# x copied into the output, and each tile's rows added into it by one accumulating scatter

## The chip, the core and the metric

The kernel runs on one core of a Trainium2 chip. The metric is the device time of one execution in microseconds (us), as the median of several runs. A profile of one execution gives, for each engine, when each instruction ran and what it waited for. The engines are PE (TensorE, matmul; its weight loads are PEld), DVE (VectorE), ACT (ScalarE), POOL (GpSimd) and SP (SyncE, which here only issues DMAs).

## What is computed

x is 4 batches of 1024 tokens with 1024 features. From x, a softmax over its rows and two outer factors (`side`, `cond`) a score is made for each of the 1024 x 1024 places of a batch, the diagonal is left out, and the 10240 highest places get a 1: that is the mask. The mask's rows are then the inputs of a mixture of eight experts, of which each token takes two, and the result is added to x:

```python
def reference(x, side, cond, G, gate_w, up_w, down_w, lora_A, lora_B):
    adj = side * cond * softmax(x) / sqrt(1024)       # diagonal: -inf
    m = ones at the 10240 highest places of each batch, else 0
    w = the two highest of softmax(m @ G), at their experts, else 0
    gated = silu(m @ gate_w[e].T) * (m @ up_w[e].T)
    out = sum over e of w[e] * (gated @ down_w[e].T + (m @ lora_A[e].T) @ lora_B[e].T)
    return x + out
```

## The kernel before

**Batches and tiles.** The four batches run one after another. A batch's 2048 pairs of token and expert are sorted by expert into T = 23 tiles of 128 slots, each tile of one expert. Since each expert's last tile is seldom full, and since 23 tiles are enough for any split, some slots hold no pair and the last tiles can be empty. While the tiles of batch n run, DVE, ACT and POOL find the mask of batch n + 1 between them, at places that tables of numbers set (`DVE_COUNT_AT`, `BELOW_AT` and others); then `route(n + 1)` on DVE makes the tables of the next batch: for each slot of each tile the row of the mask to gather (`mask_row`) and the row to write to (`put_row`).

**One tile.** POOL issues an indirect DMA that gathers 128 rows of the mask from DRAM into `xg` (`gather`, L511, three buffers, asked for three tiles ahead). PE turns them (L665), ACT stores them as `xt` (L837), PE multiplies by the first layer (L678), ACT and DVE make the gated product, PE multiplies by the second (L701 to L704), and ACT stores the result, scaled, in `y` (`store_y`, L850, two halves a tile, two buffers, NY = 2). POOL then issues an indirect DMA that writes the 128 rows of `y` to DRAM (`put_out`, L519). A slot without a pair has a row number beyond the bound, and its row is not written.

**From the put rows to the output.** `put_rows` has a row for each of the 2 x 1024 pairs of token and role (first and second expert), in two copies by turns. While batch n + 1 runs, batch n's rows are put together in 16 pieces of 128 x 512: SP loads a piece of x and the two pieces of put rows that belong to it (`load_piece`, L364 and L366), POOL adds them up (`sum_piece`, L528 and L531), and SP stores the sum in the output (`store_piece`, L373). `PIECE_AT` says after which tile POOL takes which piece. The last batch has no batch behind it: its x is loaded once more into `v`, its put rows go to the place of the first layer's weights (`last_put`, L420), DVE adds them (L1445) and SP stores the sums (L423).

**What sets the order.** Each engine takes its instructions in the written order and waits on semaphores; DMAs from SP stand in one queue, those from POOL in another. ACT waits ahead of a y store until the put of two tiles before has landed (`put`). POOL never waits for a put. SP's `move_mask(n)` waits for the mask of batch n, then loads the x of the next batch (4 MB) and stores the mask (2 MB).

Of the kernel before, what the change touches and what calls it, by code (L numbers as in the profile page):

```python
# [14 lines left out]
P = 128  # L15
# [13 lines left out]
SKIP = 4096.0  # L29
# [4 lines left out]
def build(nc, x, side, cond, G, gate_w, up_w, down_w, lora_A, lora_B, out):  # L34
# [37 lines left out]
    PIECES, NC = 2 * C, 2  # L72
# [29 lines left out]
    PIECE_AT = {**{j + 1: j for j in range(9)}, **{j + 4: j for j in range(9, PIECES)}}  # L102
    PIECES_FIRST = 14

    with ExitStack() as ctx:
# [24 lines left out]
        piece = sb("piece", [P, NC, 3, HALF], F32)  # L130
# [18 lines left out]
        spare = piece[:, :, :, :].rearrange("p i k h -> p (i k h)")  # L149
# [52 lines left out]
        none_here, second_here = temp(T), temp(T)  # L202
# [10 lines left out]
        expert_no, tile_no, token_1 = cell(E), cell(T), cell(C)  # L213
        lower = cell(E * E).rearrange("p (a e) -> p a e", a=E)
# [20 lines left out]
        def table_of(n, i, dt=F32):  # L235
# [3 lines left out]
        put_row = [table_of(n, 1, I32) for n in range(B)]  # L239
        g_scale = [table_of(n, 2) for n in range(B)]  # L240
        y_scale = [table_of(n, 3) for n in range(B)]
        expert = [table_of(n, 4, I32) for n in range(B)]
# [26 lines left out]
        put_rows = [nc.dram_tensor(f"put_rows{i}", [ROLES * S, H], F32, kind="Internal").ap() for i in range(2)]  # L269

# [24 lines left out]
        put = [sem(f"put{i}") for i in range(NY)]  # L295
        piece_landed = [sem(f"piece_landed{i}") for i in range(NC)]
        piece_stored = [sem(f"piece_stored{i}") for i in range(NC)]
        half_summed, summed_piece = sem("half_summed"), sem("summed_piece")
        last_x_landed = [sem(f"last_x_landed{c}") for c in range(C)]
        rows_landed = [sem(f"rows_landed{c}") for c in range(C)]  # L300
        last_summed, last_stored = sem("last_summed"), sem("last_stored")
# [6 lines left out]
        out_rows = out.rearrange("b (p c) h -> b p c h", c=C)  # L308
        put_roles = [a.rearrange("(r p c) h -> r p c h", r=ROLES, c=C) for a in put_rows]

        last_put = [[w1_raw[:, c, r * 2 * H:(r + 1) * 2 * H].bitcast(F32) for r in range(ROLES)]
                    for c in range(C)]
# [12 lines left out]
        def _(sp):  # L325
# [27 lines left out]
            def wait_put(n):  # L353

                for i in range(NY):
                    sp.wait_ge(put[i], 16 * len(range(i, T * (n + 1), NY)))

            def load_piece(n, j):
                u = PIECES * n + j
                at, c, half = u % NC, j // 2, j % 2  # L360
                cols = slice(half * HALF, (half + 1) * HALF)
                if u >= NC:
                    sp.wait_ge(piece_stored[at], 16 * (u // NC))
                sp.dma_start(piece[:, at, 0, :], x_rows[n][:, c, cols]).then_inc(piece_landed[at], 16)  # L364
                for r in range(ROLES):
                    sp.dma_start(piece[:, at, 1 + r, :],  # L366
                                 put_roles[n % 2][r][:, c, cols]).then_inc(piece_landed[at], 16)

            def store_piece(n, j):
                u = PIECES * n + j  # L370
                c, half = j // 2, j % 2
                sp.wait_ge(summed_piece, u + 1)
                sp.dma_start(out_rows[n][:, c, half * HALF:(half + 1) * HALF],  # L373
                             piece[:, u % NC, 0, :]).then_inc(piece_stored[u % NC], 16)
# [19 lines left out]
            for n in range(B):  # L394

                more = n + 1 < B
                if n == 0:
                    move_mask(1)
                else:
                    if n == 1:  # L400

                        sp.wait_ge(b_turned, 4)
                        sp.wait_ge(a_turned, 1)
                    wait_put(n - 1)
                    for j in range(PIECES + NC):
                        if j >= NC:
                            store_piece(n - 1, j - NC)
                        if j < PIECES:
                            load_piece(n - 1, j)
                        if more and j == PIECES_FIRST + NC - 1:  # L410
                            move_mask(n + 1)
                if n + 2 < B:
                    sp.wait_ge(scores_ready, n + 2)
                    load_t(n + 2)

            n = B - 1
            wait_put(n)
            for c in range(C):
                for r in range(ROLES):
                    sp.dma_start(last_put[c][r], put_roles[n % 2][r][:, c, :]).then_inc(rows_landed[c], 16)  # L420
            for c in range(C):
                sp.wait_ge(last_summed, c + 1)
                sp.dma_start(out_rows[n][:, c, :], v[:, c, :]).then_inc(last_stored, 16)  # L423
            sp.wait_ge(last_stored, 16 * C)
            for i in range(NC):
                sp.wait_ge(piece_stored[i], 16 * len(range(i, PIECES * (B - 1), NC)))

        @block.gpsimd
        def _(pool):
# [9 lines left out]
            nc.gpsimd.iota(token_1.bitcast(I32), pattern=[[1, C]], base=1, channel_multiplier=C)  # L439
            nc.gpsimd.iota(slot_int.bitcast(I32), pattern=[[1, P]], base=0, channel_multiplier=0)  # L440
# [7 lines left out]
            for ints in (expert_no, tile_no, token_1):  # L448
                nc.gpsimd.tensor_copy(ints, ints.bitcast(I32))
            nc.gpsimd.tensor_copy(slot_no[:, :], slot_int.bitcast(I32))  # L450
            pool.drain()
# [72 lines left out]
            def sum_piece(n, j):  # L524
                u = PIECES * n + j
                at = u % NC
                pool.wait_ge(piece_landed[at], 48 * (u // NC + 1))
                nc.gpsimd.tensor_tensor(piece[:, at, 0, :], piece[:, at, 0, :], piece[:, at, 1, :],  # L528
# [947 lines left out]
```

## Time and profile before

| | |
|---|---|
| median of 3 runs | 812.58 us (808.84 to 816.08) |
| span of the profiled execution, first to last instruction | 807.6 us |
| PE, DVE, ACT, POOL busy | 521.7, 515.2, 453.9, 390.2 us |
| DMA by SP's queue | 108.60 MB, 39.0% of 16 engines' span |
| DMA by POOL's queue | 50.37 MB, 17.9% of 16 engines' span |
| granted clock of PE, mean | 0.844 |

The profiled execution's own time is shown as this span; the median of the runs, which hold the launch's own time beside it, is 5.0 us above. Times in the rows count from the span's start. An engine's busy time is a mean over stages with different limits, so the stages are read one by one. A DMA's landing is counted from the start of the instruction that issues it to the last update of its semaphore.

### The profile page before, as it was taken

The page shows a single profiled execution, that of the slowest core. Times are in us where ns is not written, and L with a number is a line of the kernel's source. Part 1 is how long each engine was busy: PE and PEld are TensorE (multiplying, and loading weights), DVE is VectorE, ACT ScalarE, POOL GpSimd, SP SyncE. Part 2 cuts the span into 40 slices and gives each one's busy share as a digit, 9 for nine tenths or more (in the row PEclk, how much of TensorE's full clock was granted, in tenths as well). Part 3 has the DMA queues.
Part 4 walks back from the last instruction along what each step waited for, and adds up shares of the span by engine and source line. Part 5 has one row for each costly group of instructions (what it writes and reads, how often), then busy time and mean ns, then how long its engine had stood idle before and what let it go on. Part 6 is the DMA issues. An engine that isn't in the chain of part 4 may idle for free.

```text
span 807.6 us, 14610 instructions
## 1 busy us (share of the span) xinstructions
PE 521.7 (65%) x4178; PEld 356.3 (44%) x4178; DVE 515.2 (64%) x1242; ACT 453.9 (56%) x655; POOL 390.2 (48%) x337
## 2 busy tenths in 40 slices
PE   0311287179878872787889817887888278888900
PEld 0300276066545542555546515554556155555500
DVE  5768889757597675765786776657773623232345
ACT  5687387749844574387445654883456145455500
POOL 8114200115375222577887125878872168768510
PEclk9855599579999995899999958997999779999965
DMA  9990160024323553478478834685579249858469
GB/s 313 359 265 0 58 256 27 13 65 157 111 78 126 200 223 121 131 246 288 155 246 265 351 113 145 230 292 173 192 259 372 79 147 311 270 189 279 179 252 382
DMA packets 80443, 159.93 MB, mean 198 GB/s; under 512 B 22889, under 2 KB 32105, under 8 KB 79856
## 3 DMA queue, kind: packets, MB, share of 16 engines
q1 hardware_dynamic: 59760, 108.60, 39.0%
q0 software_dynamic: 20608, 50.37, 17.9%
q8 instruction: 43, 0.70, 0.3%
q14 instruction: 32, 0.26, 0.1%
HBM read 107.53 MB, written 73.40 MB: 224 GB/s over the span
## 4 chain that ended last, share of the span: by engine, by line
DMA 25%; POOL 18%; issue 15%; DVE 14%; PE 13%; ACT 7%; DVEq 3%; SPq 3%; POOLq 1%; ACTq 0%
DMA out_dram<-piece 7%; DMA piece<-put_rows 7%; DMA put_rows<-y,where 5%; POOL piece L528 4%; POOL piece L531 4%; ACT mask L793 3%; PE pa L678 3%; DMA xg<-mask_rows,where 3%; POOL xg L511 3%; POOL put_rows L519 2%; DVE w L1169 2%; DMA w<-put_rows 2%; DVE mask L1063 2%; ACT y L850 2%; PE pb L665 2%
## 5 line engine op out<-in xcount | busy, mean ns | idle before, releaser
L678 PE MATMUL pa<-w,xt 128*128 x1472 | 198.7, 289 | 1.9 <-issue 1.8
L678 PEld LDWEIGHTS pa<-w,xt 128*128 128x128 f16 x1472 | 146.8, 100 | 58.2 <-issue 12.9
L850 ACT ACTIVATE y<-pc,where 128x512 f32<-128x512 f32 x184 | 124.1, 686 | 78.9 <-PE pc L704 58.7
L511 POOL DMA_INDIRECT xg<-mask_rows,where x92 | 98.8, 1074 | 125.6 <-DVEq L1331 95.2
L519 POOL DMA_INDIRECT put_rows<-y,where x92 | 92.5, 1005 | 134.1 <-ACT y L850 112.6
L1339 DVE SCALAR_TENSOR_TENSOR g_full<-pa,where,s_act 128x144 f32<-128x144 f32 x92 | 33.6, 365 | 185.2 <-ACT s_act L842 184.8
L837 ACT ACTIVATE xt<-pb 128x1024 f16<-128x1024 f16 x92 | 94.2, 1024 | 99.0 <-PE pb L665 96.3
L665 PE MATMUL pb<-ident,xg 128*128 128x128 f16 x736 | 62.1, 233 | 68.7 <-DMA xg<-mask_rows,where 47.8
L665 PEld LDWEIGHTS pb<-ident,xg 128*128 128x128 f16 x736 | 49.2, 105 | 79.7 <-DMA xg<-mask_rows,where 53.3
L842 ACT ACTIVATE s_act<-pa,small 128x128 f32<-128x128 f32 x92 | 33.8, 368 | 87.1 <-PE pa L678 87.1
L701 PE MATMUL pc<-wd,gt 128*128 x184 | 76.0, 413 | 5.1 <-ACT y L850 4.6
L702 PE MATMUL pc<-wd,gt 128*128 x184 | 76.3, 414 | 0.0
L703 PE MATMUL pc<-wd,gt 128*128 x184 | 76.1, 413 | 0.0
L704 PE MATMUL pc<-lb,gt 128*128 x184 | 75.8, 412 | 0.0
L528 POOL TENSOR_TENSOR piece<-piece 128x512 f32<-128x512 f32 x48 | 61.3, 1277 | 24.6 <-DMA piece<-put_rows 24.1
L793 ACT ACTIVATE mask<-v,small 128x1280 f16<-128x1280 f32 x48 | 65.1, 1356 | 9.4 <-POOL v L467 6.2
L531 POOL TENSOR_TENSOR piece<-piece 128x512 f32<-128x512 f32 x48 | 62.6, 1304 | 3.8
L1347 DVE TENSOR_TENSOR g_parts<-g_full,g_parts 128x144 f16<-128x144 f32 x92 | 43.8, 476 | 6.8
L1007 DVE TENSOR_SCALAR_CACHE_REDUCE mask<-v,small 128x1024 f16<-128x1024 f32 x36 | 44.9, 1273 | 2.4 <-POOL v L467 1.6
L934 DVE TENSOR_REDUCE small<-v 128x1 f32<-128x1024 f32 x32 | 38.5, 1214 | 11.2 <-DMA v<-in_x_dram 10.8
L954 DVE SCALAR_TENSOR_TENSOR v<-v,small,t_row 128x1024 f32<-128x1024 f32 x32 | 42.8, 1376 | 0.6
L689 PE MATMUL pb<-ident,g_parts 128*128 128x128 f16 x276 | 31.8, 226 | 13.6 <-DVE gt L1355 13.4
(208 smaller groups left out, 879.2 us busy)
## 6 DMA issues: line engine op xcount, KB each, us to landing
piece<-put_rows SPq DMA_DIRECT2D x96, 256.0 KB, 3.9
v<-in_x_dram SPq DMA_DIRECT2D x40, 512.0 KB, 9.0
piece<-in_x_dram SPq DMA_DIRECT2D x48, 256.0 KB, 2.9
out_dram<-piece SPq DMA_DIRECT2D x48, 256.0 KB
mask_rows<-mask SPq DMA_DIRECT2D x4, 2048.0 KB, 17.2
w<-put_rows SPq DMA_DIRECT2D x16, 512.0 KB, 9.5
w<-in_L_ffn_gate_w_dram SPq DMA_DIRECT2D x8, 512.0 KB, 10.2
w<-in_L_ffn_up_w_dram SPq DMA_DIRECT2D x8, 512.0 KB, 8.3
```

What stands on the lines that cost most here:

```text
L511: pool.indirect_dma_start(out=xg[:, g % NX, :], out_offset=None, in_=mask_rows[n % 2], in_offset=bass.IndirectOffsetOnAxis(ap=mask_row[n][ ...
L519: pool.indirect_dma_start(out=put_rows[n % 2], out_offset=bass.IndirectOffsetOnAxis(ap=put_row[n][:, i:i + 1], axis=0), in_=y[:, g % NY, : ...
L528: nc.gpsimd.tensor_tensor(piece[:, at, 0, :], piece[:, at, 0, :], piece[:, at, 1, :], ALU.add).then_inc(half_summed, 1)
L531: nc.gpsimd.tensor_tensor(piece[:, at, 0, :], piece[:, at, 0, :], piece[:, at, 2, :], ALU.add).then_inc(summed_piece, 1)
L665: last = pe.transpose(xt_ps[:, t, :], xg[:, g % NX, t * P:(t + 1) * P], ident[:, :])
L678: last = pe.matmul(l1[g % 2], xt[:, g % 2, t, :], w1[:, bass.ds(e, 1), t, k, :].rearrange("p o n -> p (o n)"), start=(t == 0 and k == 0), ...
L701: pe.matmul(pc[:, half, :], high, own(wd[:, bass.ds(e, 1), 0, cols]), start=True, stop=False)
L702: pe.matmul(pc[:, half, :], high, own(wd[:, bass.ds(e, 1), 1, cols]), start=False, stop=False)
L703: pe.matmul(pc[:, half, :], low, own(wd[:, bass.ds(e, 1), 0, cols]), start=False, stop=False)
L793: nc.scalar.activation(mask[:, cols], v_flat[:, cols], ACT.Sign, bias=t_at[k - 1], scale=-1.0, accum_out=act_cnt[:, p:p + 1]).then_inc(act ...
L837: nc.scalar.activation(xt[:, g % 2, :, :], xt_ps, ACT.Copy).then_inc(xt_ready, 1)
L850: nc.scalar.activation(y[:, g % NY, half * HALF:(half + 1) * HALF], pc[:, half, :], ACT.Copy, scale=y_scale[n][:, i:i + 1]).then_inc(y_rea ...
```

## The change

`put_rows` and the pieces are gone. SP copies each batch's x from DRAM to DRAM into the output (`copy_x`, 4 MB each): the first two behind the last load of weights, the third and the fourth behind the loads of t_row. POOL's `put_out` becomes `add_out`: an indirect DMA that adds the 128 rows of `y` to the rows of the output (`compute_op=ALU.add`). Since two tiles can hold the same token, each of these scatters waits until the one before has landed (semaphore `added`), over all four batches in one chain; the first one of a batch waits for the copies of x too. ACT's `store_y` waits for `added` of the tile two before. A slot without a pair is no longer left out: its row of `y`, which is zero, is added to a row of its own in another batch's part of the output (`UNUSED_REGION`), so each scatter moves 128 rows. DVE makes these row numbers in `take_slots` with two instructions and one drain more. The tables of places stay as they are, without `PIECE_AT`.

```diff
-    PIECES, NC = 2 * C, 2
...
-    PIECE_AT = {**{j + 1: j for j in range(9)}, **{j + 4: j for j in range(9, PIECES)}}
-    PIECES_FIRST = 14
+    UNUSED_REGION = (1, 0, 1, 2)
...
-            def wait_put(n):
...
-            def load_piece(n, j):
...
-            def store_piece(n, j):
...
+            def copy_x(n):
+                sp.dma_start(out[n], x[n]).then_inc(x_copied[n], 16)
 
             def move_mask(n):
...
                 if n + 1 < B:
                     load_side(n + 1)
                     load_x(n + 1)
-                else:
-                    for c in range(C):
-                        sp.dma_start(v[:, c, :], x_rows[n][:, c, :]).then_inc(last_x_landed[c], 16)
...
+            copy_x(0)
+            copy_x(1)
             move_mask(0)
             sp.wait_ge(scores_ready, 1)
             load_t(1)
...
+            for n in range(1, B):
+                if n + 1 < B:
+                    copy_x(n + 1)
+                move_mask(n)
+                if n + 1 < B:
+                    sp.wait_ge(scores_ready, n + 1)
+                    load_t(n + 1)
+            sp.wait_ge(added, 16 * T * B)
...
-            def put_out(n, i):
+            def add_out(n, i):
                 g = tile(n, i)
                 pool.wait_ge(y_ready, 2 * (g + 1))
+                if i == 0:
+                    pool.wait_ge(x_copied[n], 16)
+                    pool.wait_ge(x_copied[UNUSED_REGION[n]], 16)
+                if g > 0:
+                    pool.wait_ge(added, 16 * g)
                 pool.indirect_dma_start(
-                    out=put_rows[n % 2], out_offset=bass.IndirectOffsetOnAxis(ap=put_row[n][:, i:i + 1], axis=0),
+                    out=whole_rows, out_offset=bass.IndirectOffsetOnAxis(ap=put_row[n][:, i:i + 1], axis=0),
                     in_=y[:, g % NY, :], in_offset=None,
-                    bounds_check=ROLES * S - 1, oob_is_err=False).then_inc(put[g % NY], 16)
...
+                    bounds_check=B * S - 1, oob_is_err=True, compute_op=ALU.add).then_inc(added, 16)
...
-                if n >= 2:
-
-                    pool.wait_ge(summed_piece, PIECES * (n - 1))
...
-                    if n > 0 and i in PIECE_AT:
-                        sum_piece(n - 1, PIECE_AT[i])
...
                 if g >= NY and half == 0:
-                    act.wait_ge(put[g % NY], 16 * (g // NY))
+                    act.wait_ge(added, 16 * (g - NY + 1))
...
+                V.tensor_scalar(unused_here, pair, 0.0, unused_row[:, n:n + 1], ALU.is_equal, ALU.mult)
...
-                V.tensor_copy(put_row[n], none_here)
-                V.tensor_tensor(mask_row[n], none_here, second_here, ALU.add)
+                V.tensor_tensor(none_here, none_here, second_here, ALU.add)
+                dve.drain()
+                V.tensor_copy(mask_row[n], none_here)
+                V.scalar_tensor_tensor(put_row[n], none_here, float(n * S), unused_here, ALU.add, ALU.add)
...
-            for c in range(C):
-                dve.wait_ge(last_x_landed[c], 16)
-                dve.wait_ge(rows_landed[c], 32)
-                for r in range(ROLES):
-                    last = V.tensor_tensor(v[:, c, :], v[:, c, :], last_put[c][r], ALU.add)
-                    if r + 1 < ROLES:
-                        dve.drain()
-                last.then_inc(last_summed, 1)
```

On POOL, at the fourth tile of batch 1, this stands in a row before; the diagonal of the next batch's scores is first, then a gather, a put and a piece's two adds, and the names behind "waits" are the semaphores:

```order
L467 AFFINE_SELECT v<-v 128x8x128 [waits v_scaled]
L511 DMA xg<-mask_rows,where 128x1024 [waits xt_turned]
L519 DMA put_rows<-y,where 2048x1024 [waits y_ready]
L528 TENSOR_TENSOR piece<-piece 128x512 [waits piece_landed0]
L531 TENSOR_TENSOR piece<-piece 128x512 [waits half_summed]
```

And this stands at the same place now:

```order
L414 AFFINE_SELECT v<-v 128x8x128 [waits v_scaled]
L458 DMA xg<-mask_rows,where 128x1024 [waits xt_turned]
L471 DMA out_dram<-y,where 4096x1024 [waits x_copied0,added,x_copied1,y_ready]
L458 DMA xg<-mask_rows,where 128x1024 [waits xt_turned]
L471 DMA out_dram<-y,where 4096x1024 [waits added,y_ready]
```

The adds are gone, and the indirect DMA that takes y away waits for the one before it; a gather stands between each two.

On SP, from the mask of batch 1 on, the loads and stores of pieces stood behind the load of t_row, beginning so:

```order
L388 DMA mask_rows<-mask 128x8192
L334 DMA t_row<-in_cond_dram 128x1024 [waits scores_ready]
L364 DMA piece<-in_x_dram 128x512 [waits put0,put1,a_turned,b_turned]
L366 DMA piece<-put_rows 128x512 x2
L364 DMA piece<-in_x_dram 128x512
```

Now these are all of SP's issues from the last weights to the x of batch 2 (L339 are the last weights, L316 the loads of x, L319 the load of `side`):

```order
L339 DMA spare<-in_L_ffn_lora_B_dram 128x8x16 x7
L342 DMA out_dram<-in_x_dram 64x16384 x2
L319 DMA small<-in_fside_BxSx_0_dram 128x8 [waits mask_ready]
L316 DMA v<-in_x_dram 128x1024 x8
L353 DMA mask_rows<-mask 128x8192
L322 DMA t_row<-in_cond_dram 128x1024 [waits scores_ready]
L342 DMA out_dram<-in_x_dram 64x16384
L319 DMA small<-in_fside_BxSx_0_dram 128x8 [waits mask_ready]
```

The copies of x stand where SP had nothing to issue, each as 64 runs of 16384 elements, and nothing of SP's waits for a put or a sum any more.

## Rows read from the trace of the kernel before

**Rows 1.** The page's first line.

```profile
span 807.6 us, 14610 instructions
```

**Rows 2.** Busy time of each engine in six stretches, columns named in the first line.

```profile
core 0: us, PE busy (x) PEld busy (x) DVE busy (x) ACT busy (x) POOL busy (x), PEclk, DMA share, GB/s
...
60.00:98.00 38.00, 5.48 (x16) 2.78 (x16) 32.09 (x61) 20.48 (x33) 14.17 (x7) 0.50 0.02 2
...
158.00:315.00 157.00, 118.90 (x978) 80.49 (x978) 112.29 (x297) 96.39 (x143) 60.69 (x53) 0.89 0.38 135
315.00:479.00 164.00, 123.43 (x978) 81.44 (x978) 115.43 (x297) 96.50 (x143) 102.03 (x84) 0.87 0.65 222
479.00:645.00 166.00, 122.44 (x978) 81.44 (x978) 104.95 (x287) 87.23 (x127) 103.25 (x84) 0.88 0.63 216
645.00:772.00 127.00, 106.54 (x805) 70.29 (x805) 38.18 (x115) 64.63 (x93) 86.36 (x78) 0.92 0.65 220
772.00:808.00 36.00, 0.00 (x0) 0.00 (x0) 19.61 (x16) 0.00 (x0) 0.81 (x1) 0.53 0.88 350
```

**Rows 3.** Puts L519 and gathers L511 by batch: ns min/median/max, first and last start.

```profile
L519 POOL DMA_INDIRECT put_rows<-y,where x23: 973/1015/1112, 185.5 to 301.9; - x23
...
L511 POOL DMA_INDIRECT xg<-mask_rows,where x23: 997/1024/1530, 158.0 to 265.6; - x23
...
L519 POOL DMA_INDIRECT put_rows<-y,where x23: 962/1012/1117, 342.9 to 466.1; - x23
...
L511 POOL DMA_INDIRECT xg<-mask_rows,where x23: 995/1039/1883, 314.5 to 435.8; - x23
...
L519 POOL DMA_INDIRECT put_rows<-y,where x23: 957/1000/1100, 507.4 to 632.1; - x23
...
L519 POOL DMA_INDIRECT put_rows<-y,where x23: 962/998/1123, 664.9 to 771.8; - x23
...
L511 POOL DMA_INDIRECT xg<-mask_rows,where x23: 995/1038/1048, 645.5 to 751.0; - x23
```

**Rows 4.** Landing of the puts L519 that start from 188 to 235 us.

```profile
DMA to landing us min/median/max: 3.3/3.4/3.6
```

**Rows 5.** Landing of the puts L519 that start from 292 to 305 us.

```profile
DMA to landing us min/median/max: 2.1/2.1/2.1
```

**Rows 6.** Landing of the puts L519 that start from 434 to 456 us.

```profile
DMA to landing us min/median/max: 9.5/9.9/10.2
```

**Rows 7.** Who waited for a put's landing: us in total, times, longest.

```profile
ACT y L850 <- DMA put_rows<-y,where: 19.6, 14, 2.7
```

**Rows 8.** Timeline from 766 to 808 us: start, us, engine, line.

```profile
769.80 1.27 ACT L850 ACTIVATE y<-pc,where 128x512 f32<-128x512 f32 x2 [1.77 <-DMA put_rows<-y,where]
771.84 0.96 POOL L519 DMA_INDIRECT put_rows<-y,where  x1 [2.07 <-ACT y L850]
```

**Rows 9.** Groups of the page: the first of a piece's two adds.

```profile
L528 POOL TENSOR_TENSOR piece<-piece 128x512 f32<-128x512 f32 x48 | 61.3, 1277 | 24.6 <-DMA piece<-put_rows 24.1
```

**Rows 10.** The chain of waits from 766 to 808 us: start, us, what.

```profile
781.27 16.04 DMA w<-put_rows
```

**Rows 11.** SP's issues from 0 to 160 us: start, us, line.

```profile
46.42 11.96 SPq L351 DMA_DIRECT2D piece<-in_L_ffn_lora_B_dram  x8
...
96.35 4.11 SPq L328 DMA_DIRECT2D v<-in_x_dram  x8
...
132.68 0.33 SPq L334 DMA_DIRECT2D t_row<-in_cond_dram  x1
```

**Rows 12.** DMA queues: packets, MB, share of 16 engines' span.

```profile
q0 software_dynamic: 20608, 50.37, 17.9%
```

**Rows 13.** Landing of the gathers L511 that start from 184 to 257 us.

```profile
DMA to landing us min/median/max: 2.2/3.4/3.9
```

**Rows 14.** ACT's y stores at the start of batch 3.

```profile
662.51 0.69 ACT L850 ACTIVATE y<-pc,where 128x512 f32<-128x512 f32 x1
...
675.09 0.69 ACT L850 ACTIVATE y<-pc,where 128x512 f32<-128x512 f32 x1
...
679.92 1.31 ACT L850 ACTIVATE y<-pc,where 128x512 f32<-128x512 f32 x2 [0.25 <-DMA put_rows<-y,where]
```

More of the change, by code:

```diff
@@ L28 @@
 EXPONENT = 0x7F800000
-SKIP = 4096.0
+SKIP = 8192.0
 AIM = 28.0
@@ L128, in build @@
         y = sb("y", [P, NY, H], F32)
-        piece = sb("piece", [P, NC, 3, HALF], F32)
+        spare = sb("spare", [P, 6 * HALF], F32)
         gr_parts = sb("gr_parts", [P, HT, PARTS, E], BF16)
@@ L148, in build @@
         raw_down = [wd[:, e, :, :].rearrange("p q h -> p (q h)").bitcast(F32) for e in range(E)]
-        spare = piece[:, :, :, :].rearrange("p i k h -> p (i k h)")
         raw_A = spare[:, 0:H]
@@ L213, in build @@
         expert_no, tile_no, token_1 = cell(E), cell(T), cell(C)
+        slot_row, unused_row = cell(), cell(B)
         lower = cell(E * E).rearrange("p (a e) -> p a e", a=E)
@@ L238, in build @@
         mask_row = [table_of(n, 0, I32) for n in range(B)]
-        put_row = [table_of(n, 1, I32) for n in range(B)]
+        put_row = [table_of(n, 4, I32) for n in range(B)]
         g_scale = [table_of(n, 2) for n in range(B)]
         y_scale = [table_of(n, 3) for n in range(B)]
-        expert = [table_of(n, 4, I32) for n in range(B)]
+        expert = [table_of(n, 1, I32) for n in range(B)]
         pa = ps("pa", [P, 2, 512])
@@ L267, in build @@
         mask_rows = [nc.dram_tensor(f"mask_rows{i}", [S, H], F16, kind="Internal").ap() for i in range(2)]
-        put_rows = [nc.dram_tensor(f"put_rows{i}", [ROLES * S, H], F32, kind="Internal").ap() for i in range(2)]
         x_landed = [sem(f"x_landed{c}") for c in range(C)]
@@ L294, in build @@
         gathered = [sem(f"gathered{i}") for i in range(NX)]
[L295 to L301, printed above, removed]
+        added = sem("added")
+        x_copied = [sem(f"x_copied{n}") for n in range(B)]
         xt_turned, xt_ready, l1_done, silu_done = (
@@ L307, in build @@
         x_rows = x.rearrange("b (p c) h -> b p c h", c=C)
[L308 to L312, printed above, removed]
+        whole_rows = out.rearrange("b s h -> (b s) h")
         side_rows = side.rearrange("b (p c) o -> b p (c o)", c=C)
@@ L351, in _ @@
                 sp.dma_start(raw_B[:, e, :, :], lora_B_apart[e]).then_inc(b_again, 16)
-            def wait_put(n):
-                for i in range(NY):
-                    sp.wait_ge(put[i], 16 * len(range(i, T * (n + 1), NY)))
-            def load_piece(n, j):
[L359 to L364, printed above, removed]
-                for r in range(ROLES):
-                    sp.dma_start(piece[:, at, 1 + r, :],
-                                 put_roles[n % 2][r][:, c, cols]).then_inc(piece_landed[at], 16)
-            def store_piece(n, j):
[L370 to L374, printed above, removed]
+            def copy_x(n):
+                sp.dma_start(out[n], x[n]).then_inc(x_copied[n], 16)
             def move_mask(n):
@@ L393, in _ @@
             load_t(1)
[L394 to L417, printed above, removed]
-            for c in range(C):
[L419 to L426, printed above, removed]
+            for n in range(1, B):
[6 more added lines that the diff above has]
+            sp.wait_ge(added, 16 * T * B)
         @block.gpsimd
@@ L447, in _ @@
                                     base=0, pattern=[[1, P]], channel_multiplier=-1)
-            for ints in (expert_no, tile_no, token_1):
+            for ints in (expert_no, tile_no, token_1, slot_row):
                 nc.gpsimd.tensor_copy(ints, ints.bitcast(I32))
             nc.gpsimd.tensor_copy(slot_no[:, :], slot_int.bitcast(I32))
+            pool.drain()
+            for n in range(B):
+                nc.gpsimd.tensor_scalar(unused_row[:, n:n + 1], slot_row,
+                                        float((UNUSED_REGION[n] - n) * S) - (SKIP - 1.0), None, ALU.add)
             pool.drain()
@@ L547, in _ @@
                     if i >= 3:
-                        put_out(n, i - 3)
+                        add_out(n, i - 3)
                     if n + 1 < B and i in BELOW_AT:
```

17 lines of the change are left out of this document (4 added, 13 removed).

## The prediction

> **What bounds the kernel now.** I read the stretches first [rows 2]. The four batches run one after another: 157, 164, 166 and 127 us from one batch's first gather to the next one's, and then 36 us in which PE, PEld and ACT do nothing at all and the DMA engines are 88% busy. In the batches no engine is full: in the first, PE is busy for 118.9 of 157 us, DVE for 112.3, ACT for 96.4, POOL for 60.7. The pace is set by the loop of 23 tiles that runs through all of them. The stamps of the put instructions show it [rows 3]: from the first to the last put of a batch 116.4, 123.2, 124.7 and 107.0 us pass, for 22 steps: 5.3, 5.6, 5.7 and 4.9 us a tile. The first batch has no pieces of an earlier one to sum, so 5.3 us is the pace of the tile loop with the next batch's selection in it and no pieces. Ahead of the first put stand 27.5 us after the first gather in batch 0 (158.0 to 185.5) and 19.4 us in batch 3 (645.5 to 664.9), and from the last put to the next batch's first gather it is 12.6 us (301.9 to 314.5), the routing.
>
> Then I read what a put costs, since this is what the change alters. In the quiet part of batch 0 a put of a full tile lands 3.4 us after its start [rows 4]; the three last tiles of that batch carry no rows and land after 2.1 us, which is the price of a put without data [rows 5]. Beside the bulk load of the next x and the store of the mask it is 9.5 to 10.2 us [rows 6]. In the kernel before, two puts may be in flight and POOL waits for neither: only ACT does, 14 times and for 19.6 us in all [rows 7]. So a landing time is almost wholly hidden now.
>
> Last I read the gap at POOL between a release and the issue: the last y store ends at 769.80 + 1.27 = 771.07, and the put that waits for it starts at 771.84 [rows 8]. 0.8 us goes by between the release and the start of an indirect DMA.
>
> **What goes.** The sums of the pieces on POOL go: the first of the two adds is 61.3 us of busy time [rows 9] and the second is alike, most of it beside other work. What it is worth shows in the pace: batches 1 and 2 go by 0.3 to 0.4 us a tile slower than batch 0, so 7 to 8 us a batch. In batch 3 no selection runs beside the tiles; its first four y stores come 4.2 us apart (662.5 to 675.1) until the put rows' landings hold them [rows 14], so 4.2 us is the free pace there. The closing stretch goes: after the last put at 771.8 the chain has its landing, 16 loads of put rows of which the last took 16.0 us, the sums and the stores [rows 10]. From 771.8 to 807.6 that is 35.8 us. After the change there are the landing of the last scatter and about 1 us.
>
> **What comes beside other work.** The copies of x: the two first stand on SP behind the last weight load, whose issues end at 46.4 + 12.0 = 58.4 us, and ahead of the next batch's x at 96.4 [rows 11]; between 60 and 98 us the DMA engines are 2% busy [rows 2]. 8 MB must be read and written there. By the 350 GB/s of the closing stretch [rows 2] it is 24 us, by half that, if reading and writing share it, 48 us, and then the load of x at 96.4 would come some 10 us late. I take nothing, with +10 in the range. The third copy stands behind the load of t_row at 132.7 [rows 11], in the routing of batch 0, where nothing else moves; the fourth behind the next such load, at the end of batch 0, where two or three scatters are still under way. DVE gets two small instructions and a drain more in each batch's routing, and POOL some at the start: 2 us for all, an estimate from the instructions of 0.2 us around them.
>
> **The chain.** Each scatter waits until the one before has landed. Its step is 0.8 us (release to start, [rows 8]) and then the time L from start to landing. POOL is in order: behind a waiting scatter stand the gathers, the diagonal and the `below` products. A gather is asked for three tiles ahead, and one fits into each step beside the flying scatter, so these follow the chain and don't lengthen it. ACT's store of y waits for the scatter two tiles before, so with a step above the tile pace ACT stops, and with it the whole loop: the step becomes the pace.
>
> No row shows an accumulating DMA, so L is bounded. From below: a full plain put, 3.4 us, if reading the old rows costs nothing. It costs more: all tiles now write 128 rows, the empty ones too, and each row needs the old row from DRAM besides the new one. The software queue took 17.9% of 16 engines over 807.6 us for 50.37 MB [rows 12], which is 46 us of one engine's time a MB, so 1.5 us for a tile's 0.52 MB on 16 of them. If the second stream goes through the same engines after the first, that is 3.4 + 1.5 = 4.9. The fetch from DRAM adds a delay: a gather of full tiles needs 3.4 us [rows 13], and without data 2.2, and its half as large data 0.75, so 0.45 us are left for the fetch. L = 3.4 + 1.5 + 0.4 = 5.3 us is the value I take, since the engines' own time for these bytes is the nearest row. From above: if every row is fetched, added and written before the next one is begun, the eight rows that each engine has cost 8 x (0.45 + 2 x 0.19) = 6.6 us on top of 2.1, so 8.7.
>
> The Trainium skill, Collectives: The Full Stack, in the section The bandwidth ceiling: the fold count and why AG ≠ RS ≠ AR, says that the DMA engines' add costs nothing itself, but that its two source reads halve the rate. By that rule alone L would be 2.1 + 2 x 1.5 = 5.1, the step 5.9 and the whole about 18 us less than my sum; nothing in this trace shows it.
>
> **The sum**, with a step of 0.8 + 5.3 = 6.1 us, above the free pace of 5.3 in batches 0 to 2 and 4.2 in batch 3. 22 steps are 134.2 us. Two scatters in each of batches 0 and 1 run beside the bulk load (6 MB, at 9.9 instead of 3.4, [rows 4, 6]): I add 10 us a batch, and 3 in batch 2, where only the mask's 2 MB are left. With ACT two tiles ahead of the chain, the last y is ready a step earlier against its scatter than before, and of the 12.6 us from last put to next gather about 8 are left.
> Batch 0: first scatter at 185.5, last at 185.5 + 134.2 + 10 = 329.7, next gather at 337.7 (314.5 before). Batch 1: first scatter 27.5 later at 365.2, last at 509.4, next gather at 517.4 (479 before). Batch 2: 544.9, 682.1, 690.1 (645.5). Batch 3: first scatter 19.4 later at 709.5, last at 843.7, landed at 849.0, and the end at 850; 852 with the small instructions. Against the span of 807.6 [rows 1] that is +44 us. The median of the runs, 812.6, lies 5 above this span, so I forecast 857 us.
> Each us on L moves this by 88 us (four times 22 steps), so everything hangs on L; the old time is reached at L = 4.8.
>
> **Rivals.**
> *The old rows come along almost free* (L 3.4 to 4.7). For it: a plain put at 3.4 us is 2.1 us of price without data, so delay and not bytes, and a second stream may hide in it. Against it: the 1.5 us of engine time for one stream are seen, and a second one has to go somewhere. At L = 4.0 the step is 4.8: batches 0 to 2 keep batch 0's own 156.5 us (27.5 + 116.4 + 12.6), so batch 3 begins at 158 + 3 x 156.5 = 627.5, needs 19.4 + 22 x 4.8 = 125 to its last scatter, 4 to its landing and 3 for the end and the small instructions: 760, as a median 765, faster by 6%. At L = 3.4 it is 751.
> *Near nothing*: the chain takes from the batches what the pieces and the closing stretch give: L between 4.7 and 4.9, 804 to 821 us.
> *Row after row* (L towards 8.7). For it: an add needs both rows in hand, and the engine may hold the next row back. Against it: the plain puts and gathers plainly keep several rows under way. At 8.7 the step is 9.5, 3.4 us above mine, so 88 x 3.4 = 300 us above my sum: 1157.
> The change does do what it names: in the order of instructions the put, piece and closing loads are gone, and every scatter waits for `added`.
>
> **How the numbers follow.** Chances: 0.52 for my forecast's case (L 4.9 to 7, 821 to 1000 us), 0.27 for the old rows coming free, 0.08 for near nothing, 0.13 for row after row or anything above 1000. The likeliest gives 857. The range leaves out about 0.09 below (L under 4, 765 us) and about 0.11 above (L of 6.8, 990 us); within my case alone it would be 821 to 930. A measurement of this kernel tells about 1% from no change (808.8 to 816.1 in three runs): faster 0.27, same 0.08, slower 0.65.
>
> **What would show it.** Right: scatters on POOL start one step apart, 6 us and about 0.8 us after the landing of the one before; ACT's y store waits for DMA out_dram in most tiles; from first to last scatter over 130 us in all four batches, alike in batch 3 and in batch 0; nothing after the last landing. The copies of x lie between 58 and 98 us and don't hold up the x load. Wrong: landings under 4.8 us, with the y store as what POOL waits for; or landings of 8 us and more; or copies that reach into the loads of x and shift everything before 158 us.

## The result, and the profile of the changed kernel

The changed kernel takes 949.7 us (median of 4 runs, 947.2 to 951.9) against 813.3 us before on the same chip: a ratio of 1.165, with a 95% interval of 1.160 to 1.170. The forecast was 857 us in a range of 765 to 990. Its sign was right and the time lies in the range, but the change costs 136 us where 44 were forecast.

The page of the changed kernel, its first line, its queues, its chain of waits and two of its groups:

```profile
span 950.1 us, 14369 instructions
...
q0 software_dynamic: 20608, 65.04, 38.8%
...
DMA 55%; DVE 12%; ACT 9%; issue 8%; PE 7%; POOL 5%; DVEq 3%; POOLq 1%; ACTq 0%
...
L471 POOL DMA_INDIRECT out_dram<-y,where x92 | 145.5, 1581 | 412.7 <-ACT y L787 371.7
L787 ACT ACTIVATE y<-pc,where 128x512 f32<-128x512 f32 x184 | 118.3, 683 | 337.0 <-DMA out_dram<-y,where 319.0
```

The span is 142.5 us longer than [rows 1], and more than half of the chain that ends last is DMA. The software queue took 17.9% of 807.6 us before [rows 12], 145 us; now it is 38.8% of 950.1, 369 us. The scatter is L471 now, the y store L787.

The same page's windows, by batch and with the stretch of the first copies, under the columns of [rows 2]:

```profile
60.00:98.00 38.00, 5.48 (x16) 2.78 (x16) 32.10 (x61) 20.49 (x33) 14.15 (x7) 0.50 0.68 222
158.00:368.00 210.00, 131.80 (x978) 85.06 (x978) 112.18 (x299) 94.34 (x143) 74.85 (x52) 0.80 0.57 129
...
762.00:941.00 179.00, 117.78 (x805) 73.60 (x805) 31.79 (x115) 59.83 (x93) 58.48 (x46) 0.84 0.51 90
941.00:950.00 9.00, 0.00 (x0) 0.00 (x0) 0.00 (x0) 0.00 (x0) 1.39 (x1) 0.50 0.37 58
```

The closing stretch of 36 us is 9 us, as the change promised, and POOL has 58 us in the last batch instead of 86. Yet that batch takes 179 us instead of 127 [rows 2]. Only PE and its weight loads are busier in it, by 11 and 3 us, at a granted clock of 0.84 instead of 0.92; DVE, ACT and POOL are busy for less than before. The time went into waits. The scatters' stamps, batch by batch, beside [rows 3] (ns min/median/max, then first and last start):

```profile
L471 POOL DMA_INDIRECT out_dram<-y,where x23: 1544/1582/1637, 186.3 to 364.1; - x23
...
L471 POOL DMA_INDIRECT out_dram<-y,where x23: 1552/1589/1622, 395.8 to 565.0; - x23
...
L471 POOL DMA_INDIRECT out_dram<-y,where x23: 1552/1588/1622, 596.3 to 757.8; - x23
...
L471 POOL DMA_INDIRECT out_dram<-y,where x23: 1552/1588/1622, 781.1 to 940.8; - x23
```

From first to last scatter that is 177.8, 169.1, 161.5 and 159.8 us for 22 steps, where the puts took 116.4, 123.2, 124.7 and 107.0. The instruction itself now lasts 1.58 us; a put's lasted 1.0.

The landings: of the scatters that start from 188 to 250 us, of one beside the bulk load (start 305.4) and of one beside the fourth copy of x (start 331.6), to be read beside [rows 4 to 6]:

```profile
DMA to landing us min/median/max: 5.9/6.1/6.7
...
DMA to landing us min/median/max: 11.3/11.3/11.3
...
DMA to landing us min/median/max: 18.0/18.0/18.0
```

Two scatters of batch 0 in the timeline, then the piece of the chain of waits between them (start, us, what), then the waits of the whole run (us in total, times, longest); they answer to [rows 7, 8]:

```profile
192.56 1.27 ACT L787 ACTIVATE y<-pc,where 128x512 f32<-128x512 f32 x2
193.35 1.57 POOL L471 DMA_INDIRECT out_dram<-y,where  x1 [4.04 <-ACT y L787]
199.64 1.27 ACT L787 ACTIVATE y<-pc,where 128x512 f32<-128x512 f32 x2 [4.38 <-DMA out_dram<-y,where]
200.44 1.58 POOL L471 DMA_INDIRECT out_dram<-y,where  x1 [4.16 <-ACT y L787]
```
```profile
193.35 6.21 DMA out_dram<-y,where
199.64 0.70 ACT y L787
200.34 0.10 issue
```
```profile
POOL out_dram L471 <- ACT y L787: 371.7, 79, 17.3
ACT y L787 <- DMA out_dram<-y,where: 319.0, 78, 17.6
```

Here the view must be read with care. It says that POOL waits for ACT. But the scatter at 200.44 starts in the middle of the pair of stores that runs from 199.64 to 200.91, so it cannot be sending what that pair writes: it sends the tile that was stored from 192.56 on. One landing, at 193.35 + 6.21 = 199.56, releases both: the semaphore `added` holds back this scatter and, by the two buffers, the store of the next tile's `y`. ACT needs less than 0.1 us to begin its store, POOL 0.88 us to start its DMA, and the first store of the pair ends just before that, so the profile takes it for the releaser. What POOL really waits for is the landing of the scatter before, and a step is 193.35 to 200.44: 7.1 us.

### The profile page after: what moved, and what is told of

Same layout as the page of the kernel before. It is cut to its first block, busy times and chain, and to the rows that moved or that the text cites. A ratio compares the mean times of both kernels' runs of the same rounds, so it can differ in the third digit from the quotient of the medians.

```text
span 950.1 us, 14369 instructions
## 1 busy us (share of the span) xinstructions
PE 559.5 (59%) x4178; PEld 370.0 (39%) x4178; DVE 484.0 (51%) x1234; ACT 443.1 (47%) x655; POOL 321.6 (34%) x247
## 3 DMA queue, kind: packets, MB, share of 16 engines
q0 software_dynamic: 20608, 65.04, 38.8%
## 4 chain that ended last, share of the span: by engine, by line
DMA 55%; DVE 12%; ACT 9%; issue 8%; PE 7%; POOL 5%; DVEq 3%; POOLq 1%; ACTq 0%
DMA out_dram<-y,where 52%; ACT y L787 6%; DMA xg<-mask_rows,where 3%; PE pa L615 2%; ACT mask L730 2%; DVE w L1106 2%; PE pb L602 1%; POOL out_dram L471 1%; DVE mask L1000 1%; DVE small L962 1%; POOL t_row L428 1%; DVE mask L1239 1%; DVE wd L1106 1%; DVEq L1249 1%; DVE small L871 1%
## 5 line engine op out<-in xcount | busy, mean ns | idle before, releaser
L471 POOL DMA_INDIRECT out_dram<-y,where x92 | 145.5, 1581 | 412.7 <-ACT y L787 371.7
L787 ACT ACTIVATE y<-pc,where 128x512 f32<-128x512 f32 x184 | 118.3, 683 | 337.0 <-DMA out_dram<-y,where 319.0
L602 PE MATMUL pb<-ident,xg 128*128 128x128 f16 x736 | 67.4, 245 | 129.1 <-DMA xg<-mask_rows,where 105.8
L774 ACT ACTIVATE xt<-pb 128x1024 f16<-128x1024 f16 x92 | 94.3, 1024 | 64.5 <-PE pb L602 61.9
L638 PE MATMUL pc<-wd,gt 128*128 x184 | 83.9, 456 | 48.0 <-ACT y L787 48.0
L602 PEld LDWEIGHTS pb<-ident,xg 128*128 128x128 f16 x736 | 52.5, 110 | 143.3 <-DMA xg<-mask_rows,where 114.8
L639 PE MATMUL pc<-wd,gt 128*128 x184 | 83.4, 453 | 0.0
L640 PE MATMUL pc<-wd,gt 128*128 x184 | 82.1, 446 | 0.0
L641 PE MATMUL pc<-lb,gt 128*128 x184 | 81.3, 442 | 0.0
L638 PEld LDWEIGHTS pc<-wd,gt 128*128 128x128 f16 x184 | 21.1, 115 | 67.4 <-issue 59.8
L564 PE MATMUL pd<-ident,mask 128*128 128x128 f16 x256 | 23.2, 244 | 34.7 <-ACT t_row L767 28.0
L891 DVE SCALAR_TENSOR_TENSOR v<-v,small,t_row 128x1024 f32<-128x1024 f32 x32 | 39.7, 1280 | 0.7
L721 ACT ACTIVATE v<-v,small 128x1024 f32<-128x1024 f32 x32 | 36.4, 1143 | 7.5 <-DVE small L871 7.3
```

Source lines behind the costliest of these rows:

```text
L471: pool.indirect_dma_start(out=whole_rows, out_offset=bass.IndirectOffsetOnAxis(ap=put_row[n][:, i:i + 1], axis=0), in_=y[:, g % NY, :], in ...
L602: last = pe.transpose(xt_ps[:, t, :], xg[:, g % NX, t * P:(t + 1) * P], ident[:, :])
L638: pe.matmul(pc[:, half, :], high, own(wd[:, bass.ds(e, 1), 0, cols]), start=True, stop=False)
L639: pe.matmul(pc[:, half, :], high, own(wd[:, bass.ds(e, 1), 1, cols]), start=False, stop=False)
L640: pe.matmul(pc[:, half, :], low, own(wd[:, bass.ds(e, 1), 0, cols]), start=False, stop=False)
L641: pe.matmul(pc[:, half, :], lora, own(lb[:, bass.ds(e, 1), cols]), start=False, stop=True).then_inc(y_done, 1)
```

## Experiments

The theory (A): the time is the single chain's, 22 steps a batch of issue, data, completion and release, 7.1 us each. Rival B: the DMA engines have too little time for the accumulated data, wherever a kernel waits for them. Rival C: the accumulating DMA disturbs other engines or DMAs also without a chain. Each ratio is to the kernel before on the same chip; since its medians there lie between 813.3 and 817.5 us, differences in us between runs can be off by a few us.

**The chain kept, with plain writes.**

```diff
-                    bounds_check=B * S - 1, oob_is_err=True, compute_op=ALU.add).then_inc(added, 16)
+                    bounds_check=B * S - 1, oob_is_err=True).then_inc(added, 16)
```

> The changed kernel with the chain of scatters kept, but each scatter overwrites the output's rows instead of adding to them (so the output lacks x and one of the two experts' parts). Theory A, the accumulate's landing is what costs: a plain scatter of 128 rows lands after 3.4 us again, the step is 0.9 + 3.4 = 4.3 us, below the tiles' own 5.3, so batches 0 to 2 fall back to about 156 us each and the whole to 745 to 775 us. Theory B, the single chain and the waiting POOL cost whatever the scatter does: it stays above 850 us.

769.4 us, ratio 0.943 (0.934 to 0.952) to the kernel before. The scatter's row, and its queue's:

```profile
L471 POOL DMA_INDIRECT out_dram<-y,where x92: 971/1034/2714, 185.7 to 760.2; - x92
```
```profile
q0 software_dynamic: 20608, 65.04, 23.4%
```

The same bytes, rows and chain cost 180 us less without the add. The instruction takes 1.03 us again, 0.55 less than the accumulating one, and the queue's packets 23.4% of 767.6 us, 180 us instead of 369: 189 / 92 = 2.05 us less a scatter on 16 engines.

**The add kept, without the chain.** Each tile adds into rows that no other scatter in flight touches.

```diff
-                if g > 0:
-                    pool.wait_ge(added, 16 * g)
...
-                    bounds_check=B * S - 1, oob_is_err=True, compute_op=ALU.add).then_inc(added, 16)
+                    bounds_check=B * S - 1, oob_is_err=True, compute_op=ALU.add).then_inc(put[g % NY], 16)
```

> Accumulating scatters of 128 rows, but to rows of which no two scatters in flight share one (each pair of token and expert has its own row, so the output is not the reference's), and the chain is taken away: two may be in flight, ACT waits for the one two tiles before, as in the kernel before. Theory A, the wait in the chain is what costs: two in flight give (1.5 + 0.9 + 6.2) / 2 = 4.3 us a tile, hidden below 5.3, and 750 to 785 us. Theory C, the accumulates themselves fill POOL or the DMA engines: landings grow to 10 us and more and the time stays above 880 us.

775.4 us, ratio 0.951 (0.939 to 0.962). The scatters and their landings over the whole run, and the queue:

```profile
L473 POOL DMA_INDIRECT out_dram<-y,where x92: 1544/1588/2344, 185.2 to 766.8; - x92
...
DMA to landing us min/median/max: 5.9/6.3/15.1
```
```profile
q0 software_dynamic: 20608, 65.04, 46.2%
```

Each scatter is as slow as in the changed kernel, and the DMA engines do the same work in 174 us less. So B and C fall as causes of the loss: neither the add nor the chain makes the kernel slower than before, only the two together.

**Fewer columns, chain and add kept.** With 512 and with 64 of the 1024 columns:

```diff
-        whole_rows = out.rearrange("b s h -> (b s) h")
+        whole_rows = out.rearrange("b s (q h) -> (b s q) h", q=2)
...
-                    in_=y[:, g % NY, :], in_offset=None,
+                    in_=y[:, g % NY, 0:512], in_offset=None,
```

> The chain kept, each scatter adds only the first 512 of the 1024 columns (the other half of the experts' result is left out). If the landing of 6.2 us is 1.6 issue, 8 x 0.33 = 2.6 data and 2.0 fixed, then half the data lands after 4.9 us, the step is 5.8 and the time about 835 us. If the price is one of rows, whatever their length, it lands after 5.8 us or later and the time stays above 910 us.

> The chain kept, each scatter adds only the first 64 columns of each row, 256 bytes (the rest of the experts' result is left out): what an accumulate costs nearly without data. By data and a fixed part: 1.6 + 0.2 + 2.0 = 3.8 us to landing, step 4.7, 755 to 785 us. By a price for each row: above 5 us to landing and above 880 us.

845.0 us (ratio 1.036, 1.025 to 1.047) and 771.7 us (0.946, 0.937 to 0.955). The landings of those that start from 188 to 250 us, of 512 columns and then of 64:

```profile
DMA to landing us min/median/max: 4.7/4.9/5.0
```
```profile
DMA to landing us min/median/max: 3.1/3.2/4.0
```

So a landing is 3.2 us with hardly any data, 4.9 with half and 6.1 with all. With 512 columns the landing was expected rightly and the time 10 us too short; with 64 the landing was expected at 3.8, too long. The data's share is about 3.0 us between 64 and 1024 columns, and it moves the time nearly as the sum says: from 512 to 1024 columns the landing grows by 1.2 us, 88 x 1.2 = 106, and the time by 104.7. The two don't differ in this alone: with 512 columns POOL's other work holds the chain longer, as told below under the sum, and the landings beside other transfers differ.

**Two chains of half rows.** Two scatters of 512 columns a tile, each half in a chain of its own:

```diff
-        added = sem("added")
+        added = [sem(f"added{i}") for i in range(2)]
...
+                for half in range(2):
+                    pool.wait_ge(y_ready, 2 * g + half + 1)
...
+                    if g > 0:
+                        pool.wait_ge(added[half], 16 * g)
...
+                        in_=y[:, g % NY, half * HALF:(half + 1) * HALF], in_offset=None,
+                        element_offset=half * HALF,
```

> Each tile's rows are added by two scatters of 512 columns, each half in a chain of its own, so that the second half's data may move while the first half's completion is still under way; the output is the reference's. Theory A (the change loses because the next scatter of the single chain waits for issue, data and completion of the one before it): with 512 columns one scatter lands 4.9 us after its start and the next of its chain starts 0.88 us later, so a step is 5.8 us if the two chains do not disturb one another, and at most 7.1 us if they share all of their time; at 22 steps a batch and 4 batches that takes 0 to 114 us off 949.7 us: I take a step of 6.2 us (two issues of 1.58 us lie one behind the other on GpSimd) and expect 850 to 890 us. Theory B (the DMA engines have too little time for the accumulated data, wherever it waits): the data are the same, and the time stays within 1% of 949.7 us.

879.3 us, ratio 1.079 (1.074 to 1.084): 70 us less than the changed kernel, as A expects and B doesn't. The 184 instructions and the queue:

```profile
L473 POOL DMA_INDIRECT out_dram<-y,where x184 | 293.2, 1593 | 189.7 <-ACT y L790 129.7 <-DMA out_dram<-y,where 32.6 <-issue 23.7
```
```profile
q0 software_dynamic: 33856, 65.04, 49.0%
```

A scatter of half the row takes POOL as long to issue, 1.59 us, so POOL spends 293 us on scatters instead of 146. More chains of smaller pieces would add to that; none was run.

**The copies of x moved, and nothing else.** The third goes with the first two, the fourth into the routing of batch 0.

```diff
             copy_x(1)
+            copy_x(2)
...
             load_t(1)
+            copy_x(3)
...
-                if n + 1 < B:
-                    copy_x(n + 1)
```

> The changed kernel with the copies of x moved alone (third with the first two, fourth behind the load of batch 1 during the routing of batch 0), the single chain kept; the output is the reference's. If the fourth copy cost the chain what its one slow scatter shows (18.1 us against 6.2): 12 us less than 949.7 us, so 934 to 942 us. If that scatter was late for another reason (the next batch's bulk load, which still runs there): within 3 us of 949.7 us.

938.6 us, ratio 1.149 (1.143 to 1.155), 11 us less. The scatters of batch 0 and their landings:

```profile
L471 POOL DMA_INDIRECT out_dram<-y,where x23: 1544/1582/1637, 185.7 to 352.0; - x23
...
DMA to landing us min/median/max: 5.9/6.2/11.4
```

The landing of 18.0 us is gone, and from first to last scatter batch 0 takes 166.3 us instead of 177.8. The fourth copy did cost the chain 11 to 12 us.

**A third buffer of y, and nothing else**, since ACT's 319 us of waits might be taken for the limit.

```diff
-    NX, NY = 3, 2
+    NX, NY = 3, 3
...
+        y_tiles = [y[:, 0, :], y[:, 1, :], raw_A]
```

> The changed kernel with a third buffer of y and nothing else; the single chain stays, and the output is the reference's. In its trace ScalarE waits 319 us for a free buffer. Theory A (the chain sets the pace, and that wait is only its echo): within 5 us of 949.7 us; the wait moves elsewhere by at most one tile's step of 7.1 us a batch. Rival (the two buffers of y set the pace): the tiles go back to some 6 us, 850 us or less.

943.9 us, ratio 1.156 (1.153 to 1.159). POOL's largest wait, and ACT's for a buffer:

```profile
POOL out_dram L472 <- DMA out_dram<-y,where: 170.5, 37, 8.6
```
```profile
ACT y L788 <- DMA out_dram<-y,where: 48.7, 10, 16.4
```

With y ready a tile earlier, the same wait is put down to the DMA (37 times for y and 19 for the third buffer). ACT's wait was an echo: 319.0 us become 48.7 for y and 18.1 for the third buffer, and the time moves by 6 us, just beyond the 5 of A's expectation and far from the 100 of the rival's.

**Waits only where rows can meet.** Two tiles of one expert share no token, so POOL needs to wait for the scatter before only where the expert changes, at most 7 times of 22 in a batch. DVE writes a flag for each tile, POOL loads it and branches; unused rows alternate between two sets.

```diff
-                if g > 0:
-                    pool.wait_ge(added, 16 * g)
...
+                else:
+                    with pool.If(change != 0):
+                        pool.wait_ge(put[(g - 1) % NY], 16 * ((g - 1) // NY + 1))
...
+                V.tensor_tensor(changes[n][:, 1:T], expert[n][:, 1:T], expert[n][:, 0:T - 1], ALU.not_equal)
```

> Two scatters may be in flight, and GpSimd waits for the one just before it only where the tile's expert differs from the tile before it (tiles of one expert share no token; unused rows alternate between two sets of 128), at most 7 times of 22 in a batch; the output is the reference's. Theory A (the whole loss lies in the wait of every scatter for the one before it): two in flight without any chain took 775.4 us; at most 28 waits stay, each of them some 1.5 us later than the tile's own pace, of which the second buffer of y hides most: 775 to 800 us, faster than the kernel before (813.3 us). Theory C (waits at changes of expert propagate in full, and the flag's load and branch on GpSimd cost a tile 1 us or more): 28 times 3 us and 88 times 1 us more, 860 us or above.

> As the one before, and the copies of x are moved: the third is issued with the first two, the fourth behind the load of batch 1 during the routing of batch 0, so that none runs beside scatters; the output is the reference's. Theory A: the scatter that ran beside the fourth copy landed in 18.1 us instead of 6.2, some 12 us on the chain; with two in flight part of that was hidden, so 5 to 12 us less than the kernel without the move: 765 to 790 us. Rival: the copies at the start now delay the load of the weights and scores, and the time is the same or up to 10 us longer.

803.7 us, ratio 0.986 (0.982 to 0.990), just above what A expected (775 to 800); with the copies moved 798.0 us, 0.979 (0.975 to 0.983), above the 765 to 790 expected there. Both intervals lie below 1, by only one to two and a half per cent. The rest over 775.4 seemed to lie in ACT's wait for a buffer, 139.0 us in the trace of the second against 93.1 in the run without a chain. That suggested the last version: the copies moved, three buffers of y, three sets of unused rows, and at a change of expert a wait for all that are under way.

> The version with two in flight, waits only at a change of expert, and copies of x moved, now with a third buffer of y (in the space of a loaded weight no longer needed), three sets of unused rows, and up to three scatters in flight; at a change of expert GpSimd waits for all before. The output is the reference's. If the rest over the run without any chain (798.0 against 775.4 us) lies in ScalarE's waits for a free buffer of y behind the late scatters at a change of expert: 775 to 788 us. If it lies in the flag's load and branch on GpSimd or in the data that the accumulating scatters move: 795 to 801 us.

776.4 us, ratio 0.952 (0.949 to 0.954). Its windows in batches 0 and 3, from first gather to the next batch's first gather and to the last scatter, the columns as before:

```profile
158.00:318.00 160.00, 116.79 (x978) 78.39 (x978) 114.13 (x301) 96.64 (x143) 73.76 (x52) 0.92 0.66 146
...
636.00:762.00 126.00, 106.08 (x805) 71.36 (x805) 32.35 (x115) 64.75 (x93) 58.69 (x45) 0.91 0.66 123
```

This version is 4.8% faster than the kernel before. Its ratio is that of the run without any chain (which had two buffers, and the copies where the change put them), but not batch by batch. In batch 0 first to last scatter takes 119.3 us (186.1 to 305.4) against 137.6 (185.2 to 322.8) in that run, whose fourth copy stands there. In batch 3, where neither has a copy, it is 106.3 against 95.3 (this version, then the run without a chain; another 7 of this version's scatters, from the third buffer, lie between these 16):

```profile
L483 POOL DMA_INDIRECT out_dram<-y,where x16: 1552/1588/1621, 655.8 to 762.1; - x16
```
```profile
L473 POOL DMA_INDIRECT out_dram<-y,where x23: 1552/1588/1621, 671.5 to 766.8; - x23
```

There the steps of this version reach 8.5 us, those of the other 5.9. So the waits that are left, with the flag and its branch, still take some 11 us of batch 3; the flag was not measured alone. Between the 798.0 us and this version ScalarE's wait for a buffer falls from 139.0 to 18.6 us and the time by 22; the third buffer and the third scatter in flight came together, so neither is shown alone.

## Why the prediction was right in sign and wrong in size

**What bounds the kernel, and what goes.** Right: the kernel before hid the landings, and the pieces and the closing stretch did go. The run with plain writes shows what they and the copies are worth together even with a chain: 5.7%.

**What comes beside other work.** The two first copies fit where they were put: at 60 to 98 us the DMA engines are 68% busy instead of 2%. SP's issues (start, us, line):

```profile
58.88 1.39 SPq L342 DMA_DIRECT2D out_dram<-in_x_dram  x2
...
96.54 4.39 SPq L316 DMA_DIRECT2D v<-in_x_dram  x8
...
329.98 0.52 SPq L342 DMA_DIRECT2D out_dram<-in_x_dram  x1
```

The landings of the four copies, of which the longest is the second one's:

```profile
DMA to landing us min/median/max: 15.5/16.9/27.5
```

The second copy starts at 59.7 and has landed by 87.2, so both fit ahead of the load of x, which starts at 96.5 (96.4 before, [rows 11]); the first scatter starts at 186.3 instead of 185.5. The fourth copy was named in the prediction, at the end of batch 0 "where two or three scatters are still under way", and priced at nothing; it costs 11 to 12 us. In a serial chain each of these scatters is on the path.

**The chain.** The mechanism was right: nearly all steps wait for the landing before, the pace is the step. The step that failed is the size of the term L + 0.8: "L = 3.4 + 1.5 + 0.4 = 5.3 us is the value I take". L measures 6.1 to 6.2 us, and the release 0.88 instead of 0.8: 7.1 instead of 6.1 us a step, 88 us in 88 steps. By the runs with fewer columns, 64 to 1024 columns take 3.0 us, so the whole data some 3.2, where my sum held 1.3 + 1.5 = 2.8; the second stream's engine time, 2.05 us over the run (with the collisions in it), stands for my 1.5. The fixed part is then 3.0 instead of my 2.1 + 0.4 = 2.5, and there the longer issue stands: L counts from the instruction's start, and that lasts 1.58 us instead of 1.03 with plain writes. I had given the add no price at POOL. So of the missing 0.9 us some 0.5 is fixed and 0.4 data. That the longer issue is this fixed half is read from these rows; no run varies it by itself.

The Trainium skill's rule that I had weighed (Collectives: The Full Stack, The bandwidth ceiling: the fold count and why AG ≠ RS ≠ AR) is stated there for collectives and bears on the data alone: twice 1.5 us, and the runs give 3.0 to 3.2, so they agree with it there. Of the issue it says nothing. The L of 5.1 that I had worked out from it was 1.0 us short; the longer issue is 0.55 of that, and what the rest is no run shows.

**The sum.** Against my stamps:

| term | forecast | measured |
|---|---|---|
| first scatter | 185.5 | 186.3 |
| first to last scatter, four batches | 144.2, 144.2, 137.2, 134.2 | 177.8, 169.1, 161.5, 159.8 |
| last scatter to next gather | 8 | 4.1, 4.2, 4.0 |
| last scatter to the end | 8.3 | 9.3 |
| span | 852 | 950.1 |

The second line makes 108.4 us more. 88 are the step and about 12 the fourth copy. The scatters beside the bulk loads can be read one by one; these are the landings of two in batch 0, three in batch 1 and one, beside the mask, in batch 2:

```profile
DMA to landing us min/median/max: 10.2/10.7/11.3
...
DMA to landing us min/median/max: 7.4/9.8/10.7
...
DMA to landing us min/median/max: 8.0/8.0/8.0
```

Against 6.2 us they come to 20 us, where 23 were set: that term was right. The other 11 us are small things. One start in each batch comes 1.8 to 2.4 us behind the landing before it instead of 0.88, some 5 us in all. In batch 0 this is POOL's own work: the scatter that starts at 235.39 lands at 242.05, while POOL is in a `below` product (L428), and a gather still stands ahead of the next scatter:

```profile
240.47 2.12 POOL L428 TENSOR_TENSOR t_row<-v,mask 128x1024 f32<-128x1024 f32 x1 [1.34 <-DVE small L962]
242.74 1.05 POOL L458 DMA_INDIRECT xg<-mask_rows,where  x1
244.09 1.59 POOL L471 DMA_INDIRECT out_dram<-y,where  x1 [0.30 <-issue]
```

So the gathers and `below` products do lengthen the chain here and there, which the prediction had excluded; with 512 columns, where the landings come earlier, the same start comes 4.0 us behind its landing. What is left are single landings of 6.5 to 8.1 us. The third line of the table gives 11.7 us back: I had taken too little of the overlap there.

The forecast put the median 5.0 us above the span, as the launch's own time. Each time of the changed kernel is only 1.7 to 1.8 us above its own span, and the profiled execution was the longest of the four, so the median, 949.7, lies 0.4 us below the span shown.

**The rivals.** "The old rows come along almost free" fell: no landing is under 5.8 us. "Near nothing" needed L of 4.7 to 4.9, which is what half the columns have, and with them the kernel is at 1.036. "Row after row" fell: 6.1 to 6.2 is far from 8.7. The price of the first of these can be tested all the same: at L = 3.2 (64 columns) the time is 771.7 us, where 751 stood for L = 3.4. Most of the difference is batch 0: from first to last scatter it takes 139.6 us (186.5 to 326.1) instead of 116.4, and its scatter beside the fourth copy lands after 17.5 us.

**What would show it.** One step apart, behind the landing: so, but at 7.1 us and 0.88. ACT's y store waits for the DMA in most tiles: 78 times. Over 130 us in each batch: so, but not alike; batch 0 is 18 us longer than batch 3, by the fourth copy and the bulk load. Nothing after the last landing: nothing but the program's end.

## What to carry to other kernels

A DMA whose landing is hidden behind two buffers costs little (here 19.6 us of ACT's waits, [rows 7]) until a chain makes its whole landing the pace; then price it per step, from the start of its instruction to its landing and on to the next start, and count every collision with a bulk transfer in full. Before ordering all scatters, ask which of them can meet in a row: here waits at the changes of expert, a third buffer and copies out of the way turned 16.5% slower into 4.8% faster. When the profile names an engine as the releaser, see whether the waiting instruction starts before that engine's work has ended; if so, something else released it.

## What was not expected of the hardware

- An accumulating indirect DMA holds POOL 1.58 us at its issue, a plain one with the same rows 1.03, and half as many columns don't shorten it (1.59).
- An add, which needs the old row beside the new one, does not double the landing: 6.1 us, against 3.4 for a full plain put. With next to no data it is 3.2, against 2.1 for a put without data.
- The granted clock of PE goes with the chain: 0.80 in batch 0 and 0.84 in batch 3 of the changed kernel, in whose steps PE waits, against 0.89 and 0.92 in [rows 2] and 0.92 and 0.91 in the last version. These means lie between the two granted levels, 0.5 and 1.0 of full speed. What the lower clock costs by itself no run here shows.
- Two DRAM to DRAM copies of 4 MB, issued one behind the other from 58.9 us on, had landed at 87.2: 28 us, nearer to the 24 of the forecast's bounds than to 48, and without delay to the load behind them.
